# Audio tower kernel: two stages run one after the other, against one unrolled pipeline for both

## The chip, the cores and the metric

The kernel runs on one core of one Trainium2 chip. The metric is the device time of one execution, in microseconds (us); the time before is the median of three runs. Everything else is read from one profiled execution of the same program.

## What is computed

Input `x` has 128 batch rows, 64 features and 750 time steps, all in float32. Three layers follow each other.

```python
# 1. tokens: windows of 8 steps (94 tokens), softmax over the 8 steps, weighted sum
scores = einsum('bwkf,of->bwko', xp, w) + b
pooled = sum(xp * softmax(scores, axis=2), axis=2)          # h: 128 x 94 x 64
# 2. attention, 8 heads of rank 32, on layernorm(h)
q = einsum('btd,hrd->bhtr', x, Q); k = einsum('bud,hrd->bhur', x, K)
attn = softmax(einsum('bhtr,bhur->bhtu', q, k) / sqrt(d))
ctx = einsum('bhtu,bud->bhtd', attn, x)
h = h + einsum('bhtd,hde->bte', ctx, VO)
# 3. a mixture of four experts in four heads, on layernorm(h); its code does not change
h = h + ffn(layernorm(h))
```

## The kernel before

**Units of work.** Four batch rows make a quad, so there are 32 quads (`NQUAD`). Two batch rows make a pair, whose x tile has 128 partitions (2 x 64 features) and 750 columns (375 KB). Eight pairs, or four quads, make a group (`load(G)`, 8 groups). `xs` holds two groups, so the loads of group G wait until TensorE has turned the same slots of group G - 2.

**Order.** Every engine has its own hand-written instruction list, and semaphores tie the lists together. An engine works strictly through its list, so an instruction that waits holds everything behind it. The program has three stages.

- *Tokens*, unrolled, for each quad. TensorE computes the scores of the next group's windows (`tok_score`), transposes the quad's x tiles into three PSUM banks (`turn`), and sums the weighted steps (`pool_x`). VectorE computes the softmax over the 8 steps once per group (`soft_tok`, `norm_tok`) and multiplies the three banks by the weights (`scale_x`). ScalarE copies the pooled tokens to `hj` (`store_h`). Banks 0 to 7 are all used by this stage.
- Then, once, TensorE and ScalarE make small weight products (`g_w` for the attention; `m_s`, `aq`, `wtok`, `wsx` for the experts).
- *Attention*, a software pipeline. Step g works on quads g - 4 to g + 2. The first and last steps are unrolled, and the five middle rounds of four steps are a `Fori` loop. Quads pass through: layernorm on VectorE and GpSimd (`ln_stats`, `ln_power`, `ln_apply`); `turn_x` and `project` on TensorE with copies by ScalarE (`copy_xT`, `copy_k`); three `score` products j = 0, 1, 2 of 8 matmuls each. For j = 0 and 2, VectorE takes the extreme value (`least`) and ScalarE computes eight exponentials straight from PSUM (`exp_s`, eight ACTIVATEs of 94 columns, each with its own bias). For j = 1, VectorE also subtracts, and ScalarE needs one ACTIVATE (`exp_all`). Then row sums and their reciprocals on VectorE (`sums`), the division on GpSimd (`norm_p`), a transposition on VectorE (`turn_p`), the product with the values on TensorE (`mix`), four copies by ScalarE (`copy_cT`), the output product (`give_out`), and the addition to `hj` (`add_out`).
- *Experts*, another such pipeline, which starts after the last `add_out` (`at_added` 32).

The output product reads, for each of the three token blocks j and four head pairs, one 128 x 128 block of `cT` as the stationary operand and moves the 64 columns of `vo_w` through it, in 12 matmuls a quad.
Of the kernel before, what the change touches and what calls it, by code (L numbers as in the profile page):

```python
# [13 lines left out]
KW = 8  # L14
NTOK = -(-NTIME // KW)
TP = 96
# [26 lines left out]
def audio_tower(nc, x, tok_w, tok_b, attn_q, attn_k, attn_vo, hl_w, hl_b, wq, wk, wv, gate_w, gate_b,  # L43
                ln_g, ln_b, fc1_w, fc1_b, fc2_w, fc2_b, fnorm_g, fnorm_b, fgate_w, out):
    with ExitStack() as ctx:
# [51 lines left out]
        tok_pT = sb("tok_pT", [128, TP])  # L97
        x_loaded = [sem(f"x_loaded{i}") for i in range(2 * GP)]
        x_turned = sem("x_turned")
        x_scaled = sem("x_scaled")  # L100
        x_filled = sem("x_filled")
        x_pooled = sem("x_pooled")
        h_pooled = sem("h_pooled")
        tok_scored = sem("tok_scored")
        tok_maxed = sem("tok_maxed")
        tok_biased = sem("tok_biased")
        tok_shifted = sem("tok_shifted")
        tok_exped = sem("tok_exped")
        tok_summed = sem("tok_summed")
        tok_inverted = sem("tok_inverted")  # L110
        tok_normed = sem("tok_normed")
        tok_turned = sem("tok_turned")
        tok_ready = sem("tok_ready")
# [3 lines left out]
        def tok_S(G):  # L117
            return psum[:, G % 2, 0:128]

        def tok_P():  # L120
            return psum[:, 2, 0:TP]

        def x_bank(f):
            return psum[:, 3 + f, :]

        def x_outj(Q):
            return psum[:, 6 + Q % 2, 0:3 * NFEAT]
# [20 lines left out]
        cT = sb("cT", [128, HP, NT, 4, TB])  # L148
        ln_stat = sem("ln_stat")
# [18 lines left out]
        at_cT = sem("at_cT")  # L168
        at_out = sem("at_out")
        at_added = sem("at_added")  # L170
        g_made = sem("g_made")
        g_ready = sem("g_ready")


# [6 lines left out]
        whl2 = kp[0:HD, 0, :, :, :].rearrange("o b h t -> o (b h t)")[:, 0:2 * NH * NFEAT].rearrange("o (n a f) -> o n a f", n=NH, a=2)  # L181
# [58 lines left out]
        w_made = sem("w_made")  # L240
        w_read = sem("w_read")
# [78 lines left out]
        def _(sp):  # L320

            def load(G):
                for p in range(GP):
                    slot = GP * (G % 2) + p
                    if positive(GQ * (G - 2) + p // 2 + 1):
                        sp.wait_ge(x_turned, GQ * (G - 2) + p // 2 + 1)
# [9 lines left out]

            def slow(dst, src):
# [3 lines left out]
            for n in range(NH):  # L341
                load(2 + n)
# [4 lines left out]
            load(2 + NH)  # L347
# [12 lines left out]
            load(3 + NH)  # L360
# [43 lines left out]
        def _(pool):  # L404
# [57 lines left out]
            def attention(q):  # L462
                for v in range(4):
                    g = 4 * q + v
                    if exists(g - 1, NQUAD):
                        pool.wait_ge(at_summed2, 2 * g)
                        norm_p(2)
                        pool.wait_ge(at_summed1, 2 * g)
                        norm_p(1)
# [3 lines left out]
                    if exists(g, NQUAD):  # L473
                        pool.wait_ge(at_summed0, 2 * g + 2)
                        norm_p(0)
                    if exists(g + 2, NQUAD):
                        pool.wait_ge(ln_rstd, 2 * g + 6)
                        if exists(g + 1, NQUAD):
                            pool.wait_ge(at_turned, g + 2)
# [4 lines left out]
            pool.wait_ge(h_pooled, NQUAD)  # L484
            for q in range(-1, 2):
                attention(q)
            with pool.Fori(2, 7) as q:
                attention(q)
            for q in range(7, 9):
                attention(q)  # L490

# [107 lines left out]
        def _(pe):  # L599

            def turn(G, Q, f):

                n = GQ * G + Q
                if positive(n):
                    pe.wait_ge(x_scaled, 3 * (n - 1) + f + 1)
                for i in range(4):
                    pair, c = (f, i) if f < 2 else (i // 2, 4 + i % 2)
                    mm = pe.transpose(x_bank(f)[:, 128 * i:128 * i + 128],  # L608
                                      xs[:, GP * (G % 2) + 2 * Q + pair, 128 * c:128 * c + 128], ident)
                if f == 2:  # L610
                    mm.then_inc(x_turned, 1)
                else:
                    mm.then_inc(x_filled, 1)
# [1125 lines left out]
```

## Time and profile before

| | us |
|---|---|
| median of three runs (1123.84 to 1126.86) | 1125.67 |
| time of the profiled execution | 1129.79 |
| its span, first to last instruction | 1128.0 |
| tokens, up to the last `store_h` | 0 to 144.0 |
| weight products and attention, up to the last `add_out` | 144.0 to 518.3 |
| experts | 518.3 to 1128.0 |
| TensorE, VectorE, ScalarE, GpSimd busy | 985.3, 931.5, 674.2, 676.0 |

PE is TensorE's matmul row, DVE is VectorE, ACT is ScalarE, POOL is GpSimd, SP issues the loads. The profile records each float32 matmul of this kernel as two instructions, and each transposition as one. Matmuls are pipelined, so their rows overlap; the distance from one row's start to the next row's start says how long a group holds the engine.

### The profile page before, as it was taken

How to read it: one execution, taken by the hardware profiler on the slowest of the kernel's cores; microseconds unless marked ns; L12 is line 12 of the kernel's file. 1: busy time of each engine (PE TensorE's matmuls, PEld its weight loads, DVE VectorE, ACT ScalarE, POOL GpSimd, SP SyncE). 2: the span in 40 equal slices, each digit the busy share in tenths (PEclk: the TensorE clock that was granted, in tenths of full speed). 3: DMA queues.
4: the chain of work that ended last, by engine and by line, in shares of the span. 5: the costliest groups of instructions: out<-in, count | busy, mean ns of one | idle time of the engine just before them, and what ended most of it. 6: DMA issues, size and time to landing. Idle time of an engine off the chain costs nothing.

```text
span 1128.0 us, 40703 instructions
## 1 busy us (share of the span) xinstructions
PE 985.3 (87%) x16376; PEld 681.6 (60%) x16376; DVE 931.5 (83%) x2061; ACT 674.2 (60%) x1719; POOL 676.0 (60%) x991
## 2 busy tenths in 40 slices
PE   5889878898898988986899999999999999999952
PEld 4667644454454544544677677777777776777741
DVE  3565539999999999982799999999999999999852
ACT  0111137777777777761666767767767667667621
POOL 2000036666656666541048788788888887788786
PEclk9999869999999999996899999999999999999975
DMA  7664300000000000000000001000000000010000
GB/s 256 192 207 125 113 1 2 2 2 2 1 0 0 0 0 0 2 1 6 15 10 15 16 15 23 18 16 20 14 15 19 11 20 18 12 22 19 20 8 14
DMA packets 41576, 35.31 MB, mean 31 GB/s; under 512 B 28160, under 2 KB 31232, under 8 KB 41472
## 3 DMA queue, kind: packets, MB, share of 16 engines
q1 hardware_dynamic: 41376, 33.83, 10.9%
q8 instruction: 77, 1.26, 0.5%
q14 instruction: 27, 0.22, 0.1%
q0 software_dynamic: 96, 0.00, 0.0%
HBM read 24.95 MB, written 3.08 MB: 25 GB/s over the span
## 4 chain that ended last, share of the span: by engine, by line
PE 48%; DVE 25%; POOL 12%; issue 8%; ACT 4%; DMA 1%; DVEq 1%; POOLq 0%; SPq 0%; ACTq 0%
PE psum L733 8%; DVE mx L1569 5%; PE psum L716 4%; PE psum L608 4%; PE psum L623 3%; DVE yc L1611 3%; PE psum L870 3%; PE psum L708 3%; PE psum L881 3%; PE psum L885 3%; PE psum L726 3%; POOL pu L459 3%; DVE xn L1561 2%; PE psum L855 2%; PE psum L889 2%
## 5 line engine op out<-in xcount | busy, mean ns | idle before, releaser
L459 POOL TENSOR_TENSOR pu<-pu,pr 128x752 f32<-128x752 f32 x96 | 138.7, 1444 | 127.7 <-DVE pr L1490 127.7
L524 POOL TENSOR_TENSOR st<-st,neg_half 128x12 f32<-128x12 f32 x64 | 145.8, 2278 | 5.0
L1189 ACT ACTIVATE pu<-psum,mx 128x94 f32<-128x94 f32 x512 | 124.6, 358 | 15.7 <-DVE mx L1481 14.5
L1272 ACT ACTIVATE pT<-psum 96x512 f32<-96x512 f32 (+1 forms) x224 | 126.4, 594 | 6.2 <-PE psum L870 3.3
L1569 DVE TENSOR_REDUCE mx<-psum 128x16 f32<-128x1536 f32 (+2 forms) x96 | 116.6, 1215 | 15.7 <-PE psum L855 11.5
L870 PE MATMUL psum<-ident_w,pu 128*96 128x128 f32 (+1 forms) x896 | 119.9, 275 | 1.9 <-ACT pT L1272 1.5
L1572 DVE TENSOR_TENSOR pu<-psum,mx 128x1536 f32<-128x1536 f32 (+2 forms) x96 | 117.6, 1225 | 3.3
L1266 ACT ACTIVATE pu<-pu 128x1536 f32<-128x1536 f32 (+2 forms) x96 | 101.8, 1060 | 10.0 <-DVE pu L1572 8.2
L733 PEld LDWEIGHTS psum<-vo_w,cT 128*128 128x128 f32 x768 | 90.7, 196 | 24.4 <-issue 13.0
L870 PEld LDWEIGHTS psum<-ident_w,pu 128*96 128x96 f32 (+1 forms) x896 | 100.8, 135 | 6.9 <-ACT pT L1272 4.3
L1422 DVE TENSOR_TENSOR xt<-psum,tok_pT 128x512 f32<-128x512 f32 x96 | 61.4, 684 | 50.5 <-PE psum L608 50.2
L1276 ACT ACTIVATE oc<-psum 128x336 f32<-128x336 f32 x96 | 43.2, 450 | 98.8 <-PE psum L896 96.1
L733 PE MATMUL psum<-vo_w,cT 128*128 128x64 f32 x768 | 95.2, 282 | 4.4 <-ACT cT L1198 4.3
L896 PE MATMUL psum<-gx,ct 128*128 128x84 f32 x768 | 97.9, 277 | 0.0
L896 PEld LDWEIGHTS psum<-gx,ct 128*128 128x128 f32 x768 | 90.6, 192 | 6.3 <-ACT kp L1253 6.0
L1481 DVE TENSOR_REDUCE mx<-psum 128x8 f32<-128x752 f32 x96 | 87.1, 908 | 6.7 <-PE psum L716 6.7
L445 POOL TENSOR_TENSOR ln_ve<-ln_mv,eps_c 128x3 f32<-128x3 f32 x32 | 6.2, 192 | 138.9 <-DVE ln_mv L1475 138.9
L1198 ACT ACTIVATE cT<-psum 128x384 f32<-128x384 f32 x128 | 59.6, 495 | 49.9 <-PE psum L726 49.9
L1494 DVE STREAM_TRANSPOSE pT<-pu 128x768 f32<-128x768 f32 x96 | 88.6, 948 | 0.7 <-POOL pu L459 0.7
L1488 DVE TENSOR_REDUCE pl<-pu 128x8 f32<-128x752 f32 x96 | 88.3, 920 | 1.0 <-ACT pu L1189 0.5
L716 PE MATMUL psum<-kp,xT 64*32 64x376 f32 x1536 | 83.7, 496 | 1.0 <-ACT kp L1182 1.0
L819 PE MATMUL psum<-x3T,aq 64*128 64x384 f32 x256 | 81.7, 527 | 3.1
(178 smaller groups left out, 2324.8 us busy)
## 6 DMA issues: line engine op xcount, KB each, us to landing
xs<-in_x SPq DMA_DIRECT2D x64, 375.0 KB, 4.4
vb<-va SPq DMA_DIRECT2D x32, 128.0 KB, 2.3
out_h<-ho SPq DMA_DIRECT2D x128, 16.0 KB, 1.4
out_h<-ho SPq DMA_DIRECT2D x128, 7.5 KB, 1.4
vc<-va SPq DMA_DIRECT2D x96, 16.0 KB, 1.8
gx<-in_L_ffn_gate_w SPq DMA_DIRECT2D x16, 0.2 KB
fc<-in_L_ffn_fc_w SPq DMA_DIRECT2D x12, 1.0 KB
fc<-in_L_ffn_fc_b SPq DMA_DIRECT2D x12, 0.1 KB
```

The costliest lines, as they stand in the source:

```text
L459: pool.tensor_tensor(p, p, bcast(pr[:, j, :, :].rearrange("p a b -> p (a b)"), 2, NTOK), ALU.mult).then_inc(at_normed, 1)
L524: pool.tensor_tensor(st[:, k, 3, :], st[:, k, 2, :], neg_half[:, 0:NJ * NH], ALU.pow).then_inc(rstd, 1)
L716: mm = pe.matmul(psum[TB * b:TB * b + TB, (low, high)[par], 0:HP * NTOK], xT[rows, p, b, TB * j:TB * j + TB], kp[rows, p, b, :, 0:NTOK], s ...
L733: mm = pe.matmul(psum[:, bank, NFEAT * j:NFEAT * j + NFEAT], cT[:, hp, j, :, :].rearrange("p b t -> p (b t)"), vo_w[:, hp, :], start=(hp = ...
L870: mm = pe.transpose(psum[0:rows, bank, 128 * e:128 * e + 128], src, ident)
L896: mm = pe.matmul(psum[:, bank, GC * e:GC * e + GC], ct3[:, i, 2 * (e % 2) + e // 2 if i == 1 else e, :], gx[:, e, :], start=True, stop=True)
L1189: ins = act.activation(pu[:, j, par, hp, 0:NTOK], psum[:, (low, high)[par], NTOK * hp:NTOK * hp + NTOK], ACT.Exp, bias=mx[:, j, par, hp:hp ...
L1266: act.activation(p, p, ACT.Exp).then_inc(s_exped, 1)
L1272: act.activation(pT3[j][:, f - (0, 4, 6)[i], :, :, :].rearrange("p e b t -> p (e b t)"), psum[0:rows, bank, :], ACT.Copy).then_inc(p_copie ...
L1494: dve.transpose(pT[:, j, :, :, :, :].rearrange("p a h u t -> p (a h u t)"), pu[:, j, :, :, :].rearrange("p a h u -> p (a h u)")).then_inc( ...
L1569: dve.tensor_reduce(mx3[:, i, :, :], S3(j), AX.X, ALU.max).then_inc(shifted, 1)
L1572: dve.tensor_tensor(p, S3(j), bcast(mx3[:, i, :, :], 3, QB * (j + 1)), ALU.subtract).then_inc(shifted, 1)
```

## The change

Tokens and attention become one pipeline on every engine, written out for all its 48 steps (`quad(q)` for q from -2 to 9, g = 4q + v), with no loop. In step g TensorE computes `tok_score(g + 7)`, `turn(g + 3, 0)`, `turn(g + 2, 1)`, `turn(g + 2, 2)` and `pool_x(g + 1)` among the attention work of quads g down to g - 4. The order inside a step, the distances between steps and the PSUM banks are all new. Tokens' scores have bank 0 to themselves, `tok_pT` is doubled, and the weight products are made inside steps (`make_g` at g = -4, `make_w` and `make_w2` at g = 12 and 13).

Two computations change their form. `exp_s` now also writes the row sums `pl` through `accum_out`, so `sums` of j = 0 and 2 keeps only its reciprocal. The output product is turned round: `give_outT` holds `vo_w` still and moves 192 columns of `cT`, `copy_oT` brings the transposed result to SBUF, and the new `give_out` transposes it back with six 64 x 64 products.

The loads change their order: `load(1)` comes behind the attention's weights, `load(2)` and `load(3)` among the experts' weights, and groups 4 to 7 behind all of them.

```diff
-            load(1)
             sp.dma_start(q_w[:, :, :], attn_q.rearrange("h r d -> r h d")).then_inc(attn_loaded, 16)
...
+            load(1)
+
...
-                load(2 + n)
+                if n == 0:
+                    load(2)
...
-            load(2 + NH)
+            load(3)
...
+            for G in range(4, NGROUP):
+                load(G)
...
+            def give_outT(bank):
+
+                for hp in range(HP):
+                    for half in range(2):
+                        mm = pe.matmul(psum[64 * half:64 * half + 64, bank, 0:NT * 64].rearrange("p (j c) -> p j c", j=NT), vo_w[:, hp, :],
+                                       cT[:, hp, :, 2 * half:2 * half + 2, :].rearrange("p j b t -> p j (b t)"),
+                                       start=(hp == 0), stop=(hp == HP - 1))
+                mm.then_inc(at_outT, 1)
+
             def give_out(bank):
                 for j in range(NT):
-                    for hp in range(HP):
-                        mm = pe.matmul(psum[:, bank, NFEAT * j:NFEAT * j + NFEAT], cT[:, hp, j, :, :].rearrange("p b t -> p (b t)"), vo_w[:, hp, :],
-                                       start=(hp == 0), stop=(hp == HP - 1))
+                    for half in range(2):
+                        rows = slice(64 * half, 64 * half + 64)
+                        mm = pe.matmul(psum[rows, bank, NFEAT * j:NFEAT * j + NFEAT], oT[rows, j, :, :].rearrange("p b t -> p (b t)"),
+                                       ident[rows, 64 * half:64 * half + 64], start=True, stop=True)
                 mm.then_inc(at_out, 1)
...
                         ins = act.activation(pu[:, j, par, hp, 0:NTOK], psum[:, (low, high)[par], NTOK * hp:NTOK * hp + NTOK], ACT.Exp,
-                                             bias=mx[:, j, par, hp:hp + 1], scale=-1.0)
+                                             bias=mx[:, j, par, hp:hp + 1], scale=-1.0, accum_out=pl[:, j, par, hp:hp + 1])
...
+            def copy_oT(bank):
+                act.activation(oT[:, :, :, :].rearrange("p j b t -> p (j b t)"), psum[:, bank, 0:NT * 64], ACT.Copy).then_inc(at_oT, 1)
...
-                dve.tensor_reduce(pl[:, j, :, :], pu[:, j, :, :, 0:NTOK], AX.X, ALU.add).then_inc(done, 1)
-                dve.wait_ge(done, 2 * g + 1)
+                if j in (1,):
+                    dve.tensor_reduce(pl[:, j, :, :], pu[:, j, :, :, 0:NTOK], AX.X, ALU.add).then_inc(done, 1)
+                    dve.wait_ge(done, 2 * g + 1)
                 dve.reciprocal(pr[:, j, :, :], pl[:, j, :, :]).then_inc(done, 1)
```

The order of a full step is set by the new `quad(q)` of each engine. Three waits in it tie the engines together where the prediction speaks of them. On TensorE, `mix` of quad g - 3 waits for both `exp_s` of quad g - 2 (they free banks 1 and 2) and for `least(1)` of quad g - 2 (it frees banks 4 and 5); `score(0)` of quad g - 1 needs the four `kp` copies of that quad, two of which follow the `project` that follows `mix`. On ScalarE, `exp_s(0)` waits for `least(0)` (`at_maxed0`).

```diff
+                    if exists(g - 3, NQUAD):
+                        pe.wait_ge(at_pturned, 3 * g - 6)
+                        if exists(g - 2, NQUAD):
+                            pe.wait_ge(at_exped, 3 * g - 4)
...
+                        if exists(g - 2, NQUAD):
+                            pe.wait_ge(at_maxed1, 2 * g - 2)
...
+                        mix((v + 1) % 4, (1, 2, 4, 5))
...
+                    if exists(g - 1, NQUAD):
+                        pe.wait_ge(at_q, 4 * g)
...
+                        score((v + 1) % 2, 0, 6, 7)
```

TensorE before, first a quad of the tokens stage (L608 transposes x, L623 scores tokens, L635 pools), in the unrolled part of the program.

```order
8 L608 MATMUL psum<-ident_w,xs 128x128 x12
9 L623 MATMUL psum<-xs,tw 32x128 x12
10 L635 MATMUL psum<-xt,pick 32x192 x8
11 L608 MATMUL psum<-ident_w,xs 128x128 x12
12 L635 MATMUL psum<-xt,pick 32x192 x8
```

TensorE before, a full step of the attention (L702 `turn_x`, L716 `score`, L708 `project`, L733 `give_out`, L726 `mix`).

```order
142 L702 MATMUL psum<-ident_w,xn 128x128 x3
143 L716 MATMUL psum<-kp,xT 32x376 x8
144 L708 MATMUL psum<-xT,g_w 128x384 x2
145 L716 MATMUL psum<-kp,xT 32x376 x8
146 L733 MATMUL psum<-vo_w,cT 128x64 x12
147 L716 MATMUL psum<-kp,xT 32x376 x8
148 L726 MATMUL psum<-pT,xn 64x384 x24
149 L708 MATMUL psum<-xT,g_w 128x384 x2
```

TensorE of the change, one full step (L706 `give_outT`, L680 `project`, L624 `tok_score`, L698 `mix`, L715 the new `give_out`, L612 `turn`, L632 `pool_x`, L688 `score`, L674 `turn_x`).

```order
71 L706 MATMUL psum<-cT,vo_w 64x192 x8
72 L680 MATMUL psum<-xT,g_w 128x384 x2
73 L624 MATMUL psum<-xs,tw 32x128 x12
74 L698 MATMUL psum<-pT,xn 64x384 x24
75 L680 MATMUL psum<-xT,g_w 128x384 x2
76 L715 MATMUL psum<-ident_w,oT 64x64 x6
77 L612 MATMUL psum<-ident_w,xs 128x128 x4
78 L632 MATMUL psum<-xt,pick 32x192 x8
79 L688 MATMUL psum<-kp,xT 32x376 x8
80 L674 MATMUL psum<-ident_w,xn 128x128 x3
81 L612 MATMUL psum<-ident_w,xs 128x128 x8
82 L688 MATMUL psum<-kp,xT 32x376 x16
```

The token work of one quad now stands between the attention products of other quads, and the first `score` of a quad stands behind `mix`, `project`, `give_out`, `turn` and `pool_x`.

ScalarE before, one full step of the attention (L1189 the exponentials, L1182 `kp` copies, L1198 `cT` copies, L1195 `exp_all`, L1178 `xT`).

```order
52 L1189 ACTIVATE pu<-psum,mx 128x94 x8
53 L1182 ACTIVATE kp<-psum 128x4x96
54 L1189 ACTIVATE pu<-psum,mx 128x94 x8
55 L1198 ACTIVATE cT<-psum 128x3x4x32 x2
56 L1182 ACTIVATE kp<-psum 128x4x96 x2
57 L1195 ACTIVATE pu<-pu 128x8x94
58 L1198 ACTIVATE cT<-psum 128x3x4x32
59 L1178 ACTIVATE xT<-psum 128x3x4x32
60 L1198 ACTIVATE cT<-psum 128x3x4x32
61 L1182 ACTIVATE kp<-psum 128x4x96
```

ScalarE of the change, one full step (L1286 the exponentials with their sums, L1279 `kp`, L1292 `exp_all`, L1300 `copy_oT`, L1295 `cT`, L1258 `store_h`, L1275 `xT`).

```order
81 L1275 ACTIVATE xT<-psum 128x3x4x32
82 L1286 ACTIVATE pu,pl<-psum,mx 128x94 x16
83 L1279 ACTIVATE kp<-psum 128x4x96
84 L1292 ACTIVATE pu<-pu 128x8x94
85 L1300 ACTIVATE oT<-psum 128x192
86 L1279 ACTIVATE kp<-psum 128x4x96
87 L1295 ACTIVATE cT<-psum 128x3x4x32 x2
88 L1279 ACTIVATE kp<-psum 128x4x96 x2
89 L1295 ACTIVATE cT<-psum 128x3x4x32 x2
90 L1258 ACTIVATE hj<-psum 128x192
```

The sixteen exponentials of a quad now stand in one piece, each with a second output, and two copies of 192 columns are new in the step.

## Rows read from the trace of the kernel before

**Rows 1.** Busy time by stage: tokens, attention, experts

```profile
11.30:144.00 132.70, 115.04 (x1684) 92.59 (x1685) 74.00 (x151) 14.23 (x48) 0.00 (x0) 0.92 0.55 170
144.00:518.30 374.30, 325.41 (x4265) 179.37 (x4261) 326.22 (x672) 266.58 (x837) 216.80 (x256) 0.95 0.00 1
518.30:1128.00 609.70, 544.83 (x10432) 409.68 (x10432) 527.64 (x1216) 392.07 (x833) 452.70 (x704) 0.95 0.08 16
```

**Rows 2.** Timeline of PE, one attention step: start, duration, group, idle before

```profile
344.29 0.86 PE L716 MATMUL psum<-kp,xT 64*32 64x376 f32 x16
345.08 2.89 PE L733 MATMUL psum<-vo_w,cT 128*128 128x64 f32 x24
347.90 0.86 PE L716 MATMUL psum<-kp,xT 64*32 64x376 f32 x16
348.72 2.19 PE L726 MATMUL psum<-pT,xn 32*64 32x384 f32 x48
350.85 0.92 PE L708 MATMUL psum<-xT,g_w 64*128 64x384 f32 x4
352.94 0.54 PE L702 MATMUL psum<-ident_w,xn 128*128 128x128 f32 x3 [1.18 <-POOL xn L454]
...
354.21 0.92 PE L708 MATMUL psum<-xT,g_w 64*128 64x384 f32 x4
355.06 0.86 PE L716 MATMUL psum<-kp,xT 64*32 64x376 f32 x16
```

**Rows 3.** The same step: span, busy PE, PEld, DVE, ACT, POOL, clock, DMA

```profile
344.29:355.06 10.77, 9.60 (x134) 5.20 (x132) 10.21 (x23) 8.29 (x26) 6.77 (x8) 1.00 0.00 0
```

**Rows 4.** Timeline of PE, one quad of the tokens stage

```profile
75.00 1.53 PE L608 MATMUL psum<-ident_w,xs 128*128 128x128 f32 x12
76.46 0.97 PE L623 MATMUL psum<-xs,tw 128*32 128x128 f32 x21
...
77.34 0.84 PE L635 MATMUL psum<-xt,pick 128*32 128x192 f32 x15
78.11 1.53 PE L608 MATMUL psum<-ident_w,xs 128*128 128x128 f32 x12
```

**Rows 5.** Groups of instructions, VectorE and ScalarE, tokens stage: busy, mean ns, idle

```profile
L1422 DVE TENSOR_TENSOR xt<-psum,tok_pT 128x512 f32<-128x512 f32 x96 | 61.4, 684 | 50.5 <-PE psum L608 50.2
...
L1402 DVE TENSOR_TENSOR tok_e<-tok_e,tok_r 96x128 f32<-96x128 f32 x8 | 2.3, 286 | 0.3
...
L1148 ACT ACTIVATE hj<-psum 128x192 f32<-128x192 f32 x32 | 10.6, 330 | 93.5 <-PE psum L635 93.5
```

**Rows 6.** Groups of instructions, VectorE, 200 to 480 us

```profile
L1488 DVE TENSOR_REDUCE pl<-pu 128x8 f32<-128x752 f32 x78 | 71.7, 919 | 0.0
L1481 DVE TENSOR_REDUCE mx<-psum 128x8 f32<-128x752 f32 x78 | 70.9, 909 | 0.0
```

**Rows 7.** Timeline of ScalarE, one attention step

```profile
345.21 1.95 ACT L1189 ACTIVATE pu<-psum,mx 128x94 f32<-128x94 f32 x8 [0.32 <-DVE mx L1481]
347.00 0.54 ACT L1182 ACTIVATE kp<-psum 128x384 f32<-128x384 f32 x1
```

**Rows 8.** ScalarE's group of exponentials over the run: duration min, median, max

```profile
L1189 ACT ACTIVATE pu<-psum,mx x512: 330/357/471, 163.0 to 499.4; 128x94 f32<-128x94 f32 x171
```

**Rows 9.** Timeline of ScalarE in the experts stage, its smallest instruction

```profile
710.69 0.20 ACT L1296 ACTIVATE fe<-fl 128x12 f32<-128x12 f32 x1
710.79 0.97 ACT L1253 ACTIVATE kp<-psum 128x384 f32<-128x384 f32 x2
```

**Rows 10.** Timeline of PE at the start of the tokens stage

```profile
11.38 6.10 PE L623 MATMUL psum<-xs,tw 128*32 128x128 f32 x96 [11.38 <-DMA tokb<-in_L_tok_b]
19.86 0.42 PE L643 MATMUL psum<-ident_w,tok_e 96*128 96x96 f32 x1 [2.38 <-DVE tok_e L1402]
```

**Rows 11.** Timeline of PE at the end of the attention

```profile
492.59 1.50 PE L716 MATMUL psum<-kp,xT 64*32 64x376 f32 x32 [0.97 <-ACT kp L1182]
```

**Rows 12.** Timeline of DVE, the last addition to `hj`

```profile
517.91 0.36 DVE L1499 TENSOR_TENSOR hj<-psum,hj 128x192 f32<-128x192 f32 x1 [10.28 <-PE psum L733]
```

More of the change, by code:

```diff
@@ L482, in attention @@
                         ln_apply(g + 2, (v + 2) % 4)
[L484 to L490, printed above, removed]
+                    if exists(g, NQUAD):
+                        pool.wait_ge(at_summed1, 2 * g + 2)
+                        norm_p(1)
+            for q in range(-2, 10):
+                quad(q)
             def power3(g):
@@ L665, in _ @@
-            pool_x(NQUAD - 1)
-            pe.wait_ge(x_scaled, 3 * NQUAD)
-            pe.wait_ge(tok_ready, NGROUP)
-            pe.wait_ge(attn_loaded, 16 * 4)
-            for half in range(2):
-                for i in range(2):
-                    for par in range(2):
-                        hd = 2 * (2 * i + half) + par
-                        mm = pe.matmul(psum[64 * half:64 * half + 64, 0, 64 * (2 * i + par):64 * (2 * i + par) + 64],
-                                       k_w[:, hd, :], q_w[:, hd, :], start=True, stop=True)
@@ L793, in attention @@
-                    if exists(g + 1, NQUAD):
-                        score((v + 1) % 2, 0, 4, 5)
-                    if exists(g + 2, NQUAD):
-                        pe.wait_ge(at_xT, g + 3)
-                        project(v % 2, 0, 0, 2)
-                    if exists(g + 1, NQUAD):
-                        score((v + 1) % 2, 2, 6, 7)
-            pe.wait_ge(h_pooled, NQUAD)
-            for q in range(-1, 2):
-                attention(q)
-            with pe.Fori(2, 7) as q:
-                attention(q)
@@ L806, in _ @@
-            for q in range(7, 9):
-                attention(q)
+                            pe.wait_ge(at_xT, g)
+                        score((v + 1) % 2, 2, 1, 2)
+                    if g + 4 == 0:
+                        pe.wait_ge(tok_ready, ((g + 4) // 4) + 1)
+                        make_g()
+            for q in range(-2, 10):
+                quad(q)
             pe.wait_ge(causal_set, 10)
@@ new lines, in quad @@
+                    if exists(g - 2, NQUAD):
+                        act.wait_ge(at_maxed2, g - 1)
+                        exp_s(2, 1, 2)
+                    if exists(g - 1, NQUAD):
+                        act.wait_ge(at_pb, g)
+                        copy_k((v + 1) % 2, 2, 6)
+                    if exists(g - 2, NQUAD):
+                        act.wait_ge(at_maxed1, 2 * g - 2)
+                        exp_all(1)
+                    if exists(g - 4, NQUAD):
+                        act.wait_ge(at_outT, g - 3)
+                        copy_oT(3)
@@ L1244, in front_xT @@
+                    if exists(g - 3, NQUAD):
+                        copy_cT(1, 2)
+                    if g + 3 == 0:
+                        if exists(g + 3, NQUAD):
+                            act.wait_ge(g_made, 1)
+                        copy_g()
+                    if exists(g - 3, NQUAD):
+                        copy_cT(2, 4)
+            for q in range(-2, 10):
+                quad(q)
             def front_xT(bank):
```

654 lines of the change are left out of this document (371 added, 283 removed).

## The prediction

> **What bounds the kernel now.** I first cut the span into its three stages [rows 1]. Tokens take 132.7 us after TensorE's first matmul at 11.38 us, attention 374.3 us, experts 609.7 us. The change leaves the experts' code alone, so their 609.7 us stay; what can move is the 518.3 us before them. The reader should see that the two stages have opposite habits. In the tokens stage TensorE is busy 115 of 132.7 us, VectorE 74, ScalarE 14 and GpSimd 0. In the attention all four work, but the stage starts empty and ends empty.
>
> A full attention step [rows 3] lasts 10.77 us. VectorE is busy 10.21 of it, TensorE 9.60, ScalarE 8.29, GpSimd 6.77. TensorE's timeline [rows 2] gives each group by start-to-start distances: a `score` 0.80, `give_out` 2.82, `mix` 2.13, a `project` 0.85, `turn_x` 0.47, and one gap of 1.18 us in which it waits for the layernorm. So VectorE and TensorE bound the step together. With 32 quads at 10.77 us the stage would take 345 us; the other 30 us are the weight products, filling and draining.
>
> In the tokens stage a quad needs 3.11 us of TensorE [rows 4]: transposes 1.46, `tok_score` 0.88, `pool_x` 0.77. VectorE's `scale_x` waits 50.2 us for TensorE there and works 61.4 us [rows 5]. The loads move 170 GB/s at a DMA share of 0.55 [rows 1], so they are not the bound even now; spread over the whole pipeline they need well under half of that rate.
>
> **TensorE after.** Per step: 9.60 without the old output product (2.82) is 6.78. Add the tokens' 3.11. The new output product isn't in the trace; `give_outT` has 8 matmuls that move 192 columns. The nearest row is `pool_x`, also 8 matmuls of 192 columns, which takes 0.77 us with four column quarters side by side, that is two rounds. `give_outT` has two column halves, four rounds: 1.5 us. Below, 1.3; above, if the halves did not run beside each other, eight rounds, 3.1. The new `give_out` has 6 products of 64 x 64 in pairs; the old one took 2.82 / 12 = 0.235 us a matmul, so 0.5, between 0.35 (three pairs at half that) and 1.4. Sum 6.78 + 3.11 + 1.5 + 0.5 = 11.9 us a step.
>
> **VectorE after.** 10.21, minus two row sums of 0.92 [rows 6], plus three `scale_x` of 0.684 [rows 5], plus a group's six small softmax instructions of about 0.29 each [rows 5] over four quads, 0.4: 10.8 us. Below TensorE.
>
> **ScalarE after.** 8.29, plus `store_h` 0.33 [rows 5], `copy_oT` of the same width 0.33, the tokens' exponential and copy 0.15: 9.1, plus 16 times the price a of a summed exponential. The trace has no `accum_out`. Without it eight exponentials take 1.79 us start to start [rows 7], 0.224 each, though each lasts 0.357 [rows 8]: neighbours overlap by 0.133. Sums leave the engine's accumulator by an extra write. The smallest ScalarE instruction [rows 9] has 12 columns, lasts 0.20, and the next starts 0.10 after it. So a lies between 0 (no instruction of its own) and 0.33 (0.20 for the write, and the lost overlap 0.133). I take 0.15, between the 0.10 that the row costs its neighbour and the 0.20 that it lasts. ScalarE's load is then 11.5 us a step.
>
> The Trainium skill, "ScalarE: Activation LUTs", section "What ACT_TABLE_LOAD costs", puts an ACTIVATE with immediate operands at 186 ns plus 0.83 ns a column, with 93 ns of overlap between neighbours. If the sum's write is such an instruction of one column, a would be an estimated 0.09 us by that page and the step about 1 us shorter than my sum has it; its 186 ns agree with the 0.20 row [rows 9].
>
> **The loop that sets the step.** Loads alone give 11.9. But the new order ties TensorE and ScalarE into a ring. `exp_s(0)`, `exp_s(2)` of quad g - 2 must end before `mix` of quad g - 3 (it takes their banks). Behind `mix` stand `project`, `give_out`, `turn`, `pool_x`, and only then `score(0)` of quad g - 1, then `least(0)`, then the next `exp_s(0)`. Length: exponentials 16 x 0.224 + 16 x 0.15 = 5.98; `mix` 2.13; `project` 0.85; `give_out` 0.5; `turn` of four transposes 1.46 / 3 = 0.49; `pool_x` 0.77; `score` 0.80; `least` 0.91 [rows 6]; three hand-offs between engines at 0.1 (the exponentials wait 0.32 from the start of their idle time for `least` [rows 7], the most that I would allow in sum). That is 12.7. Every fourth step VectorE has the group's softmax ahead of `least(0)` and ScalarE an exponential, about 1.1 us, 0.3 a step. The step is 13.0 us: TensorE waits 1.1 of it in front of `mix`. Queued behind `mix` is all of the above, the `cT` copies and VectorE's `least(0)`; nothing else fills that time, since TensorE's list is fixed.
>
> **The sum.** The start is as before up to the first group's transposed weights, 19.86 [rows 10]; the weight product for the attention follows at once. Then steps g = -3 to 0 are short chains (transposes, `scale_x`, `pool_x`, layernorm), 1.5 + 3 + 4 + 7 us, to about 36. Step 1 adds `project`, the `kp` copies and two scores, 8 us; step 2 the exponentials, 11; step 3 `mix`, 12: full steps begin near 67. Steps 4 to 24 are full, 21 x 13.0 = 273. Steps 25 to 31 lose `tok_score`, the group softmax and later the turns, but keep the ring: 7 x 12.7 = 89. Step 32 has no new quad, 10.5. Then the last quad drains. Before, from the end of the last `score` pair at 494.1 [rows 11] to the last addition's end at 518.27 [rows 12] took 24.2 us; the new output product is shorter and the granted clock as low, 22. Sum 67 + 273 + 89 + 10.5 + 22 = 461.5, against 518.3: 56.8 us less. The weight products of 9 us hide in steps 12 and 13 but for a little, which the sum takes as nothing (their cover is the wait ahead of `mix`; without it, 3 us more). From the profiled execution's 1129.8 that leaves 1073.0. The median of the runs shown is 4.1 us below that execution, so I predict 1069 us.
>
> **Moved DMAs.** The attention's four weight loads now stand before the second group, whose first pair is needed right behind the attention product at about 22 us; a few us of delay there are inside the range. Slots come free three steps, over 30 us, before they are needed again, so later loads are hidden, and the small experts' loads behind `load(3)` are needed only in step 12.
>
> **Rivals.**
> - *The ring is short and TensorE bounds* (the summed exponentials cost 0.10 or less): 11.9 to 12.1 a step. 28 steps x 1.0 less: 1069 - 28 = 1041. For it: the 0.10 of [rows 9]. Against it: a write that reads what the instruction before it has just summed may not overlap like two strangers. Chance 0.2.
> - *The ring is longer*, with a at 0.20 (0.8 us a step), or `give_outT`'s halves one after the other (TensorE 13.5), or VectorE late with `least(0)`, since its own load leaves 2 us: 13.6 to 14.8 a step, 1086 to 1119. Chance 0.2.
> - *Slower than before*: the sum's write waits for its exponential to end and the next waits for the write, a = 0.33. The ring is 13.0 + 16 x 0.18 = 15.9 us, 28 x 2.9 = 81 us more: 1150. It decides from a = 0.28, where the step is 15.0 and the gain of 57 us is spent. Against it: the neighbours of [rows 7] overlap although each has its own bias. Chance 0.07.
> - *The pipeline gains nothing from the merge* since TensorE's instructions, now unrolled, arrive late while x is loaded: the tokens stage was unrolled too, with the loads at a share of 0.55, and TensorE was busy 115 of 132.7 us [rows 1]. Chance 0.02, about 1125.
>
> **How the numbers follow.** The forecast, a step of 12.4 to 13.6 us (1052 to 1086), has a chance of 0.48; its own range is that. 0.03 is left for a step that is still shorter or a faster start. The range takes in the TensorE-bound case and most of the longer ring: 1037 to 1105. What a measurement of this kernel can tell from no change is about 0.3%, 3.4 us. Faster by over 0.3%: 0.91; within it 0.02; slower 0.07.
>
> **What would show it.** The experts' start near 462 us (518.3 before) and their length unchanged; a step of 13.0 us between two `mix` groups; TensorE idle about 1 us ahead of `mix`, released by ScalarE's exponentials; eight summed exponentials in 3.0 us; `give_outT` 1.5 us. Wrong would be: a step under 12.2 with TensorE never waiting, a wait for VectorE ahead of `score` or the exponentials, or `give_outT` near 3.

## The result and the profile after

| | before | after |
|---|---|---|
| median of four executions | 1124.97 us | 1058.18 us |
| their spread | 1123.84 to 1126.86 | 1055.77 to 1060.38 |
| profiled execution, its own time | 1129.8 us | 1060.38 us |
| its span | 1128.0 us | 1058.6 us |
| start of the experts stage | 518.3 us | 446.1 us |

The changed kernel is faster, ratio 0.940 (95% interval 0.938 to 0.943). It came out 11 us below the forecast of 1069 us, inside its range.

First, from the page of after, the two groups of a summed exponential, then the group of `mix` (columns: busy, mean ns, idle before and its releaser).

```profile
L1286 ACT ACTIVATE pu<-psum,mx 128x94 f32<-128x94 f32 x512 | 164.6, 374 | 4.5 <-DVE mx L1583 2.3
...
L1286 ACT ACTIVATION_READ_ACCUMULATOR pu<-psum,mx 128x1 f32 x512 | 123.8, 242 | 0.0
...
L698 PE MATMUL psum<-pT,xn 32*64 32x384 f32 x1536 | 72.6, 502 | 22.0 <-ACT pu L1286 22.0
```

A summed exponential is two instructions: the ACTIVATE and a read of the accumulator, 512 of each. And all that TensorE waits ahead of `mix` in the whole run, 22.0 us, it waits for these exponentials.

Next, a full step of after between two `mix` groups, the stretch in one row (the columns are those of [rows 3]), then the chain of waits through the same step.

```profile
250.05:262.17 12.12, 11.78 (x188) 6.70 (x188) 10.52 (x24) 10.19 (x45) 6.73 (x8) 1.00 0.20 65
```

```profile
250.05 2.19 PE psum L698 x48
252.25 0.84 PE psum L680 x4
253.09 0.49 PE psum L715 x12
253.59 0.59 PE psum L612 x4
254.18 0.79 PE psum L632 x16
254.96 0.88 PE psum L688 x16
...
255.86 0.95 DVE mx L1583
...
256.84 5.24 ACT pu L1286 x32
262.08 0.09 issue
262.17 2.19 PE psum L698 x48
```

Reading down: `mix`, `project`, `give_out`, `turn`, `pool_x`, `score(0)`, `least(0)`, sixteen summed exponentials, the next `mix`. This is the ring of the prediction, member for member, and it lasts 12.12 us. TensorE is busy 11.78 of it, so it is only 0.34 short of being the bound itself. Two `mix` groups are 12.12 apart in all but a few of the full steps; every fourth is 12.35, and one of these is 18.62 (the weight products). The 0.23 us more of the fourth step is one member more in the ring, TensorE's `tok_turn` between `pool_x` and `score(0)`:

```profile
230.50 0.23 PE psum L637
```

The price of a sum is read from ScalarE's timeline, start to start.

```profile
256.84 0.34 ACT L1286 ACTIVATE pu<-psum,mx 128x94 f32<-128x94 f32 x1
257.07 0.19 ACT L1286 ACTIVATION_READ_ACCUMULATOR pu<-psum,mx 128x1 f32 x1
257.17 0.33 ACT L1286 ACTIVATE pu<-psum,mx 128x94 f32<-128x94 f32 x1
...
261.87 0.57 ACT L1279 ACTIVATE kp<-psum 128x384 f32<-128x384 f32 x1
```

Sixteen take 261.87 - 256.84 = 5.03 us, 0.314 each, against 0.224 without the read [rows 7]. The read lasts 0.19 to 0.29 us, but the exponential behind it starts 0.10 after the read's start: a = 0.09. The estimate that the prediction worked out from the Trainium skill, "ScalarE: Activation LUTs", section "What ACT_TABLE_LOAD costs" (186 ns less 93 ns of overlap), was 0.09 too. The trace agrees on that distance; the read itself lasts longer than 186 ns, 241 ns in the median of all 512.

`give_outT`, on TensorE's timeline of that step:

```profile
258.46 1.52 PE L706 MATMUL psum<-cT,vo_w 128*64 128x192 f32 x16
259.91 0.92 PE L680 MATMUL psum<-xT,g_w 64*128 64x384 f32 x4
```

`give_outT` takes 1.45 from its start to the next group's, the new `give_out` 0.49 (in the chain above), together 1.94 where the old product took 2.82 [rows 2].

Last, VectorE's last addition to `hj`, which answers to [rows 12]: its end at 446.09 is where the experts start.

```profile
445.73 0.36 DVE L1602 TENSOR_TENSOR hj<-psum,hj 128x192 f32<-128x192 f32 x1 [3.48 <-PE psum L715]
```

### The profile page after: what moved, and what is told of

It is laid out like the page before. It is cut to its first block, busy times and chain, and to the rows that moved or that the text cites. A ratio compares the mean times of both kernels' runs of the same rounds, so it can differ in the third digit from the quotient of the medians.

```text
span 1058.6 us, 41021 instructions
## 1 busy us (share of the span) xinstructions
PE 945.7 (89%) x16504; PEld 641.0 (61%) x16504; DVE 881.5 (83%) x1997; ACT 723.9 (68%) x2263; POOL 675.7 (64%) x991
## 3 DMA queue, kind: packets, MB, share of 16 engines
q8 instruction: 95, 1.56, 0.6%
## 4 chain that ended last, share of the span: by engine, by line
PE 42%; DVE 24%; ACT 16%; POOL 8%; issue 7%; DMA 1%; DVEq 1%; POOLq 0%
ACT pu L1286 15%; PE psum L698 7%; DVE mx L1685 5%; DVE yc L1727 3%; PE psum L985 3%; PE psum L996 3%; PE psum L1000 3%; PE psum L688 3%; DVE mx L1583 3%; PE psum L680 3%; PE psum L1004 3%; DVE xn L1677 2%; PE psum L970 2%; PE psum L632 2%; PE psum L612 2%
## 5 line engine op out<-in xcount | busy, mean ns | idle before, releaser
L472 POOL TENSOR_TENSOR pu<-pu,pr 128x752 f32<-128x752 f32 x96 | 138.7, 1445 | 137.8 <-DVE pr L1593 137.8
L1286 ACT ACTIVATE pu<-psum,mx 128x94 f32<-128x94 f32 x512 | 164.6, 374 | 4.5 <-DVE mx L1583 2.3
L1286 ACT ACTIVATION_READ_ACCUMULATOR pu<-psum,mx 128x1 f32 x512 | 123.8, 242 | 0.0
L1597 DVE STREAM_TRANSPOSE pT<-pu 128x768 f32<-128x768 f32 x96 | 92.9, 970 | 7.6 <-PE psum L698 5.0
L698 PE MATMUL psum<-pT,xn 32*64 32x384 f32 x1536 | 72.6, 502 | 22.0 <-ACT pu L1286 22.0
L1696 DVE SCALAR_TENSOR_TENSOR ct<-sxT,psum 128x512 f32<-128x512 f32 x96 | 65.2, 680 | 24.1 <-PE psum L1004 17.3
L688 PE MATMUL psum<-kp,xT 64*32 64x376 f32 x1536 | 76.2, 487 | 2.7 <-ACT xT L1275 1.6
L1295 ACT ACTIVATE cT<-psum 128x384 f32<-128x384 f32 x128 | 55.9, 497 | 26.4 <-PE psum L698 26.4
L970 PE MATMUL psum<-kp,sxT 32*32 32x256 f32 (+2 forms) x3072 | 69.3, 390 | 0.0
```

The source lines that it names most:

```text
L472: pool.tensor_tensor(p, p, bcast(pr[:, j, :, :].rearrange("p a b -> p (a b)"), 2, NTOK), ALU.mult).then_inc(at_normed, 1)
L688: mm = pe.matmul(psum[TB * b:TB * b + TB, (low, high)[par], 0:HP * NTOK], xT[rows, p, b, TB * j:TB * j + TB], kp[rows, p, b, :, 0:NTOK], s ...
L698: mm = pe.matmul(psum[64 * par:64 * par + 64, banks[b], 0:HP * TP], xn[rows, r, ub, 0, :], pT[rows, :, par, :, ub, :], start=(ub == 0), st ...
L1286: ins = act.activation(pu[:, j, par, hp, 0:NTOK], psum[:, (low, high)[par], NTOK * hp:NTOK * hp + NTOK], ACT.Exp, bias=mx[:, j, par, hp:hp ...
```

## The experiments

Nine kernels ran, and the changed kernel once more (changed_again). Times differ a little from chip to chip, so each is given as a ratio to the kernel before on the same chip. The steps are distances between two `mix` groups in one profiled execution of each.

| kernel | full step | group's step | ratio | 95% interval |
|---|---|---|---|---|
| changed kernel | 12.12 | 12.35 | 0.9404 | 0.9379 to 0.9429 |
| no_sums | 11.79 | 12.02 | 0.9246 | 0.9208 to 0.9283 |
| sums_on_vector | 12.76 | 14.8 to 16.3 | 0.9716 | 0.9666 to 0.9766 |
| old_product | 12.58 | 14.04 | 0.9581 | 0.9544 to 0.9619 |
| merge_alone | 12.58 | 14.57 | 0.9658 | 0.9641 to 0.9675 |
| sums_alone (old stages) | 10.77 | | 1.0017 | 1.0001 to 1.0034 |
| late_pool | 11.97 | 12.68 | 0.9366 | 0.9328 to 0.9403 |
| late_w | 12.12 | 12.35 | 0.9340 | 0.9322 to 0.9358 |
| late_w_late_pool | 11.97 | 12.69 | 0.9346 | 0.9325 to 0.9367 |
| late_split | 12.12 | 12.35 | 0.9363 | 0.9348 to 0.9379 |
| changed_again | 12.13 | 12.37 | 0.9388 | 0.9375 to 0.9401 |

### Is it the ring through ScalarE? (no_sums)

The row sums of j = 0 and 2 are left out, and the softmax's denominators are 1 there.

```diff
-                                             bias=mx[:, j, par, hp:hp + 1], scale=-1.0, accum_out=pl[:, j, par, hp:hp + 1])
+                                             bias=mx[:, j, par, hp:hp + 1], scale=-1.0)
...
+            dve.memset(pl[:, :, :, :], 1.0).then_inc(zeroed4, 1)
```

> Edit: the changed kernel with the exponentials' accum_out taken away and nothing in its place (the row sums of j = 0 and 2 are a constant 1, so the division of these rows is left out of the result). It prices the summed exponentials. Theory A (the ring from the exponentials over mix, project, give_out, turn, pool_x, score and least back to the exponentials sets the step of 12.12 us): the ring loses 16 x 0.09 = 1.44 us and would be 10.7, so TensorE's own load of 11.8 sets the step; 28 to 31 steps x 0.33 less, 9 to 10 us: 1048 us. Theory B (TensorE's load already sets the step, and its wait of 0.34 ahead of mix is only a hand-off): no change, 1058 us. In the trace A wants TensorE's wait ahead of mix gone and the step at 11.8.

Measured: 1042.82 us, ratio 0.9246. The stretch between two `mix` groups:

```profile
242.57:254.36 11.79, 11.78 (x188) 6.70 (x188) 10.51 (x23) 9.02 (x29) 6.75 (x8) 1.00 0.21 67
```

The step is TensorE's load to 0.01 us, and nothing waits ahead of `mix`. So the ring binds with the sums and TensorE without them, and the two are 0.33 us apart. The reads put 16 x 0.09 = 1.44 us into the ring but cost 0.33 a step, because the rest lay under TensorE's load. The time is 5 us under theory A's 1048. Of the 18.8 us between the two spans, 12.2 lie between the first and the last `mix` (the last two distances gain 1.2 and 1.6, not 0.33), 3.2 ahead of the first, and 3.2 in the experts. These last 3.2 are not the sums' work: the experts' code is the same, and their time varies by that much from execution to execution (below).

### The same sums on VectorE (sums_on_vector)

```diff
-                if j in (1,):
-                    dve.tensor_reduce(pl[:, j, :, :], pu[:, j, :, :, 0:NTOK], AX.X, ALU.add).then_inc(done, 1)
-                    dve.wait_ge(done, 2 * g + 1)
+                dve.tensor_reduce(pl[:, j, :, :], pu[:, j, :, :, 0:NTOK], AX.X, ALU.add).then_inc(done, 1)
+                dve.wait_ge(done, 2 * g + 1)
```

The exponentials lose their `accum_out` as in no_sums, and the counts in GpSimd's waits follow.

> Edit: the changed kernel with the row sums of j = 0 and 2 back on VectorE (two reductions of 0.93 us a step), exponentials without accum_out. Theory A (each engine's load bounds when the ring is short): VectorE's 10.52 us becomes 12.38, so the step is 12.4 to 12.7 and the time 1066 to 1075 us. Theory B (only the ring counts, and it gets 1.44 us shorter while VectorE's added work hides): TensorE bounds at 11.8, 1048 us.

Measured: 1097.72 us, ratio 0.9716, slower than forecast. The row of a step, and the VectorE part of its chain:

```profile
270.99:283.75 12.76, 11.78 (x188) 6.69 (x188) 12.13 (x25) 9.02 (x29) 6.74 (x8) 1.00 0.18 61
```

```profile
276.80 0.94 DVE mx L1583
277.74 1.20 DVE xt L1532 x2
...
280.77 0.83 DVE pl L1590
...
282.66 0.95 DVE pu L1586
```

VectorE now has 12.13 us of work in 12.76, and the ring runs through its list from `least(0)` to the next `mix`; no exponential is in it. A plain step loses only 0.64 us. Between the first and the last `mix` the kernel takes 44.0 us more than the changed kernel. The plain steps are 10 of them. The last nine steps are 13: six `mix` groups there took 3.5 to 3.9 us instead of 2.19, at the lower clock. The largest part, 21, is in the group's steps, which last 14.8 to 16.3 where the changed kernel takes 12.35 (and 22.8 for 18.62 with the weight products).

Two things make the group's steps long. VectorE has nothing spare for the group's softmax, and one instruction of it, `tok_mb` on a tile of 96 x 16, lasts 1.39 us here where it lasts 0.23 in the changed kernel. GpSimd's `norm_p` (L472) runs beside it and ends 0.02 us before it. First sums_on_vector, VectorE's row and GpSimd's, then the changed kernel:

```profile
245.21 1.39 DVE L1509 TENSOR_SCALAR tok_mb<-tok_m,tokb 96x16 f32<-96x16 f32 x1
245.14 1.44 POOL L472 TENSOR_TENSOR pu<-pu,pr 128x752 f32<-128x752 f32 x1
```

```profile
226.13 0.23 DVE L1509 TENSOR_SCALAR tok_mb<-tok_m,tokb 96x16 f32<-96x16 f32 x1
```

The two group's steps of 14.8 us ran at the full clock, those of 16.3 did not: in the second row below TensorE took 3.72 us from the first `score` to the end of `turn` (mean granted clock 0.55), in the first 2.15.

```profile
243.38:258.22 14.84, 12.26 (x188) 6.75 (x189) 14.52 (x31) 9.23 (x31) 6.78 (x8) 1.00 0.17 54
349.64:365.92 16.28, 12.79 (x165) 7.04 (x165) 14.82 (x31) 9.19 (x31) 6.78 (x8) 0.90 0.00 2
```

### The old output product in the new pipeline (old_product)

```diff
-                        give_outT(3)
+                        give_out(3)
...
-                    for half in range(2):
-                        rows = slice(64 * half, 64 * half + 64)
-                        mm = pe.matmul(psum[rows, bank, NFEAT * j:NFEAT * j + NFEAT], oT[rows, j, :, :].rearrange("p b t -> p (b t)"),
-                                       ident[rows, 64 * half:64 * half + 64], start=True, stop=True)
+                    for hp in range(HP):
+                        mm = pe.matmul(psum[:, bank, NFEAT * j:NFEAT * j + NFEAT], cT[:, hp, j, :, :].rearrange("p b t -> p (b t)"), vo_w[:, hp, :],
+                                       start=(hp == 0), stop=(hp == HP - 1))
...
-                        copy_oT(3)
```

The old call of `give_out(7)` between `project` and `turn` goes, and VectorE's `add_out` moves to the end of its step, since the sum is there later.

> Edit: the changed kernel with the old output product (12 matmuls, cT stationary) at give_outT's place in the step, into bank 3; copy_oT and the six turning products are gone, and add_out stands at the end of VectorE's step. TensorE's load is 11.78 - 1.45 - 0.49 + 2.82 = 12.66 us, while the ring loses 0.49. Theory A (two bounds, the longer one sets the step): step 12.7, 0.55 us x 28 to 31 more, 1073 to 1076 us. Theory B (only the ring counts): step 11.6 to 11.8, 1044 to 1049 us.

Measured: 1080.89 us, ratio 0.9581. The row of a step:

```profile
264.07:276.65 12.58, 12.58 (x187) 7.80 (x184) 10.35 (x22) 9.98 (x44) 6.80 (x9) 1.00 0.19 62
```

TensorE is busy through the whole step, and later, where `tok_score` has ended, the step falls to 11.64. This is plain TensorE bound: the new product takes 0.80 us off TensorE's load (12.58 to 11.78), which puts it under the ring, and the step gains 0.46 of that. The time is 5 to 8 us above theory A's, and the group's steps, which A left out, are the larger part of that: each is 1.46 us longer than a plain one. TensorE stands at `tok_turn` there for the end of VectorE's softmax, in which `tok_mb` lasts 1.49 us beside `norm_p`, 1.26 more than in the changed kernel.

### The merge alone, and the sums alone

merge_alone is the pipeline with the edits of sums_on_vector and old_product together, so with neither companion computation. sums_alone is the kernel before, in its two stages, with this edit only (and the counts in GpSimd's waits that follow from it):

```diff
-                                             bias=mx[:, j, par, hp:hp + 1], scale=-1.0)
+                                             bias=mx[:, j, par, hp:hp + 1], scale=-1.0, accum_out=pl[:, j, par, hp:hp + 1])
...
+                if j in (1,):
+                    dve.tensor_reduce(pl[:, j, :, :], pu[:, j, :, :, 0:NTOK], AX.X, ALU.add).then_inc(done, 1)
```

> The one pipeline with neither companion edit: all row sums on VectorE and the old output product at its old place. Theory A: VectorE's load is the one of sums_on_vector (12.1 busy in a step of 12.77), TensorE's that of old_product (12.58), and the two form one ring without ScalarE's accumulator: 12.9 to 13.6 us a step, with group steps of 15 to 16; 1090 to 1110 us, ratio 0.97 to 0.985. Theory B: the merge is where nearly all of the gain is, the rest is small: as old_product, ratio 0.955 to 0.965.

> The kernel before with one edit: the row sums of j = 0 and 2 come with ScalarE's exponentials, all else as it was (two stages). Theory A: VectorE (10.21 busy of 10.77) was the nearer bound of the attention step and loses 1.84; ScalarE gains 16 x 0.09 = 1.4 to 9.7, TensorE stays at 9.6: the step falls to 9.7 to 10.1, 32 x 0.8 = 26 us less, ratio 0.973 to 0.98. Theory B: TensorE's wait of 1.18 us for the layernorm stays because the ring there runs through the exponentials as well, which are 1.4 longer: step 10.6 to 10.8, ratio 0.995 to 1.0.

Measured: merge_alone 1088.26 us, ratio 0.9658; sums_alone 1128.39 us, ratio 1.0017, no gain. A step of merge_alone, then one of sums_alone:

```profile
267.15:279.73 12.58, 12.58 (x187) 7.80 (x184) 12.01 (x26) 8.70 (x28) 6.74 (x8) 1.00 0.19 62
```

```profile
337.29:348.06 10.77, 9.59 (x140) 5.16 (x132) 8.65 (x19) 9.63 (x44) 6.80 (x9) 1.00 0.00 0
```

merge_alone's ratio lies at the border of theory B's range, and A had its plain step wrong: it is TensorE's 12.58, not VectorE's. In sums_alone VectorE has lost 1.56 us of work and the step has not moved (10.77). The chain of waits through its step tells why, and it holds no VectorE and no ScalarE work at all:

```profile
339.82 0.51 POOL xc L450
...
340.41 0.98 POOL xn L454 x2
341.39 0.12 issue
341.51 0.54 PE psum L702 x3
...
344.49 2.82 PE psum L733 x24
347.31 0.79 PE psum L716 x16
348.10 2.22 PE psum L726 x48
```

The old step was TensorE's 9.59 and 1.18 of waiting for GpSimd's `xc` and `xn`, which start behind the end of `mix`. Both theories for sums_alone had a wrong picture: A took VectorE for the nearer bound, B put the exponentials into the ring. It also shows what the merge did: its plain step of 12.58 is all TensorE, so the 1.18 went to token work.

Four kernels with the pipeline make a square. With the old product the sums on ScalarE bring 0.8% (0.9658 to 0.9581). With the new product they bring 3.1% (0.9716 to 0.9404). With the sums on ScalarE the new product brings 1.8%. With the sums on VectorE it brings nothing: 0.9716 against 0.9658, with plain steps of 12.76 against 12.58. These ratios hold the group's steps and the stretches at the lower clock too. The plain steps alone say the same: 12.58 with either place of the sums under the old product, 12.76 and 12.12 under the new one. The new product puts `give_out` between `mix` and `score(0)`, into the ring, so TensorE's shorter list pays only if the ring has room for it.

### The order inside the step (late_pool)

`pool_x` and `tok_turn` go from ahead of the first `score` to behind it.

```diff
+                    if exists(g - 1, NQUAD):
+                        pe.wait_ge(at_q, 4 * g)
...
+                        score((v + 1) % 2, 0, 6, 7)
                     if exists(g + 1, NQUAD):
                         pe.wait_ge(x_scaled2, g + 2)
...
-                        score((v + 1) % 2, 0, 6, 7)
```

> Edit: the changed kernel with pool_x and tok_turn moved behind the first score of the step on TensorE; no work is added or taken away. Theory A (the ring sets the step): pool_x's 0.79 us leave the ring, VectorE's transposition and scale_x then hold least back, so the ring is 11.3 to 11.7 and TensorE's load of 11.8 sets the step: 9 to 10 us less, 1048 us. Theory B (TensorE's load sets it already): no change, 1058 us.

Measured: 1056.25 us, ratio 0.9366: the median is under the changed kernel's 0.9404, but the intervals overlap, so the step tells more. The chain of its step:

```profile
253.12 0.83 PE psum L688 x16
253.96 0.79 PE psum L632 x16
254.74 0.49 PE psum L674 x3
...
255.26 0.49 ACT xT L1275
255.75 5.13 ACT pu L1286 x32
```

`pool_x` was 0.79 us of the ring, but only 0.15 came off (11.97), and the group's step grew to 12.68. `score(0)` is early now, and still `pool_x` and `turn_x` are in the ring, since ScalarE's list has the copy of `xT` ahead of the exponentials. An instruction comes out of a ring only where it leaves every engine's list between two members.

### The weight products (late_w, late_split)

late_w moves `make_w` to step 33 and `make_w2` behind the last step; VectorE's `split_w` goes to step 30. late_split is late_w with `split_w` in step 32.

```diff
-                    if g + 3 == 16:
-                        if exists(g - 13, NQUAD):
-                            pe.wait_ge(w_read, 1)
-                        make_w2()
...
+                    if g == 33:
+                        pe.wait_ge(tok_ready, NGROUP)
+                        pe.wait_ge(w_split, 1)
+                        make_w()
...
+            pe.wait_ge(w_read, 1)
+            make_w2()
```

> The expert weight products (the two tiny ones and the sixteen small ones), which stand inside step 12 to 13 of the changed kernel, are moved behind the last score, where TensorE waits for ScalarE in the drain. Theory A: the one step of 18.6 us there is 6.5 us longer than its neighbours because nothing in the ring covers the products, and in the drain part of them fills waits of 3.5 to 3.7 us: the step falls to 12.1 to 12.4, the drain grows by 0 to 2 us, total 4 to 6 us under the changed kernel, ratio to the kernel before 0.935 to 0.937. Theory B: the products' time is only moved (the drain grows by 5 to 6 us, since the last quad's chain waits behind them): ratio as the changed kernel's, 0.939 to 0.942.

> Both moves at once: weight products behind the last score, and tokens' pooling and turning behind the attention's first score. If the two savings are of different places they add: about 3 us (late_pool) and 5 us (late_w) under the changed kernel, ratio to the kernel before 0.931 to 0.934. If the later score makes ScalarE's list late in the drain, only the larger remains: 0.935 to 0.937.

late_w_late_pool has the edits of late_w and of late_pool.

> As late_w, with VectorE's preparation of the expert weights (split_w: two copies and two subtractions, 2.47 us) at step 32 and not at step 30. Theory A: in late_w this work stood ahead of VectorE's turn_p(2), scale_x and least(0), so TensorE waited 1.30 us for scale_x, that step took 14.1 us, and the granted clock fell to 0.56 in the next mix (3.80 us for 2.13): step 32 has no scale_x left, so 2 to 3.5 us come back, ratio to the kernel before 0.931 to 0.933. Theory B: the clock falls anyway in this part and the delay only moves to step 32: as late_w, 0.934.

> The changed kernel once more, beside late_split and in the same rounds of the kernel before, as the mark for the small differences of the last runs: ratio 0.938 to 0.942 as measured first. If it is at 0.942 or above on this chip, late_w's and late_pool's gains are larger than read so far, if under 0.937 they are not told from nothing.

Measured: late_w 0.9340, late_w_late_pool 0.9346, late_split 0.9363 beside changed_again's 0.9388. The long step is gone in all three. Between the first and the last `mix`, late_w takes 373.3 us, late_split 371.5 and late_w_late_pool 371.4, against 377.4 in the changed kernel. What late_w gave back is in its chain, ahead of the exponentials of one of the last steps:

```profile
381.35 0.07 DVE whl L1530
381.42 0.66 DVE whl L1531
382.08 1.33 DVE whl L1530
383.41 0.32 DVE whl L1531
```

`split_w` itself, 2.5 us with its last instruction, stands between the addition to `hj` and `least(0)`. That step took 14.08 us, and the `mix` behind it ran at the lower clock (3.80 us instead of 2.19, below). More than half of the 2.5 us is the copy of 16 x 4 elements that takes 1.33: `norm_p` runs beside it, and it ends 0.02 us behind `norm_p`. In late_split the chain through step 32 has the same copy of 1.33 us on it, at 403.73 us.

So theory A of late_split was wrong in its place: `split_w` is not off the path there, where the step takes 13.40 us instead of 11.36. The delay of 2.0 us only moved, as B has it, and what came back, 1.8 us between the first and the last `mix`, answers to the `mix` that kept the full clock (1.6 us). These are differences of single traces: by its median late_split has a ratio of 0.9363, above both theories' figures and not told from late_w's 0.9340 (the intervals overlap). Against changed_again on the same chip it is 1052.42 to 1056.83 us, 0.4% less. The sixteen small products behind the last step were not free either, since the experts' first product waits behind them. It starts 3.17 us after the last addition in the changed kernel, 4.02 in late_split and 5.56 in late_w, where the second half of the products ran at the lower clock; VectorE then waits 2.81 us instead of the usual 1.2. late_w's experts take 614.3 us and late_split's 610.9, but how much of that is the products is not shown, since this time varies by 3.7 us without them (below). The savings of late_w and late_pool add between the first and the last `mix` (4.1 and 1.9 us, together 6.0), not in the total, where the experts of that execution took 615.2 us. The versions between 0.934 and 0.937 are a little faster than the changed kernel; which of them is best these runs can't tell.

## Why the prediction was nearly right, step by step

It forecast 1073.0 us for the profiled execution and 1069 for the median; they are 1060.4 and 1058.2.

- **"The loop that sets the step": right.** The chain shows it member for member. Only `tok_turn`, 0.23 us in every fourth step, is missing from it. The step was 12.12 us and not 13.0, which lies below the forecast's own range of 12.4 to 13.6. The step of the prediction that failed is the price a of a summed exponential, taken as 0.15 "between the 0.10 that the row costs its neighbour and the 0.20 that it lasts". It measured 0.09: -0.96 us a step. What counts is the lower of these, the distance to the neighbour. The estimate from the Trainium skill's page was the better one, and the prediction set it aside.
- **The other members of the ring** were 0.35 us too short in sum: `turn` 0.59 for 0.49, `score` 0.88 for 0.80, the last exponential's whole length, less one hand-off. Only the last ends of a group count in a ring, and they are longer than the start-to-start distances that I added up.
- **The group's softmax** was put at 0.3 us a step. It cost nothing: VectorE had 1.6 us of room in the step (10.52 busy of 12.12). The 0.23 us of every fourth step, 0.06 a step, are `tok_turn`'s.
- **TensorE's load** was forecast at 11.9 and is 11.78; `give_outT` 1.5 and 1.45, `give_out` 0.5 and 0.49. VectorE 10.8 and 10.52. ScalarE 11.5 and 10.19, 0.96 of the 1.31 from a.
- **"The weight products of 9 us hide ... the sum takes as nothing": wrong.** That step is 18.62 us, 6.5 more than its neighbours. On TensorE's timeline the sixteen small products run from 179.89 to 183.56 and their forerunner (L654) takes 0.88, 4.55 us in all. The cover was the wait ahead of `mix`, which is 0.34 and not the 1.1 of the forecast. And the next stretch, `score` and `give_outT`, ran at a granted clock of 0.56 and took 3.83 us where it takes 2.16 in the step shown above. The forecast's other value, 3 us without cover, was too low as well:

```profile
179.89 0.43 PE L661 MATMUL psum<-m_s,whl 16*128 16x64 f32 x2
...
183.56 1.50 PE L688 MATMUL psum<-kp,xT 64*32 64x376 f32 x16
184.99 2.47 PE L706 MATMUL psum<-cT,vo_w 128*64 128x192 f32 x16
```

```profile
183.56:187.39 3.83, 3.83 (x34) 1.84 (x33) 2.19 (x5) 3.23 (x19) 0.46 (x1) 0.56 0.00 0
```

- **"VectorE and TensorE bound the step together" (of the kernel before): wrong.** sums_alone shows it. It was TensorE and GpSimd's `xn`; VectorE's 10.21 of 10.77 was load beside the path. This sentence didn't enter the sum, so it cost the prediction nothing, but it would have misled whoever had tried the sums alone first.
- **The sum by stretches.** The first 68.7 us (67 forecast), 21 full steps 262.2 (273; 6.5 of them the weight products), seven steps 83.4 (89), the rest 31.8 (32.5): 446.1 against 461.5. The experts took 612.5 and not 609.7. From 1003 to 1012 us TensorE ran at a granted clock of 0.50 there, in changed_again, whose experts took 610.2, at 1.00. In the eight other executions that have the same experts' code and nothing new ahead of it they took 609.2 (late_pool) to 612.9 us (sums_alone), so this is spread. It did hide a fifth of the error.
- **The rivals.** "TensorE bounds", 11.9 to 12.1 a step, is nearer to what came than the forecast's ring: the ring is 0.34 above TensorE's load. Its condition, a of 0.10 or less, was met; its 1041 us wasn't, since the ring then is 12.1 and not under 11.9, and since the weight products stood open. no_sums is that rival in pure form: 1042.8 us. That the time fell into the forecast's own range owes something to errors of opposite sign: -0.9 us a step, +6.5 for the weight products, +2.8 for the experts.

Open: why TensorE's clock fell in four of the six group's steps of sums_on_vector and not in the two of 14.8 us, whose waits are the same 0.85 and 0.59 us. A late `pool_x` together with the copy of `xT` behind the exponentials, which late_pool's chain points to, wasn't tried.

## What to carry to other kernels

When in-order engines hand work round, write the ring down with each engine's list between two members, and compare its length with each load: here they were 0.34 us apart, so each half of the change pays in full only with the other (the sums 0.8% alone and 3.1% with the new product, the new product nothing alone and 1.8% with the sums). An engine at 95% of a step need not bound it: take work away from it alone and look, as in sums_alone, or read the chain of waits rather than the busy shares. Work taken as hidden needs a named cover of its size on each engine; where the cover is a wait that the same change shortens, price the work in full. A merged order also sets which instructions of two engines run side by side: look for one whose duration has grown, as `tok_mb`'s from 0.23 to 1.39 us.

## What the runs showed of the hardware

A sum through `accum_out` is an instruction of its own, which lasts 0.19 to 0.29 us and costs 0.09 between neighbours of 94 columns, though it reads what the one before it has just summed.

VectorE's `tok_mb`, 96 x 16, lasts 0.23 us wherever `norm_p` does not run beside it. In all 18 places where it does (six each in sums_on_vector, old_product and merge_alone) it lasts 1.13 to 1.50 and ends 0.02 to 0.04 us after `norm_p`, whichever of the two started first. That it waits for GpSimd's instruction is read from these ends; no run moved that instruction alone.

TensorE's granted clock fell from full speed to 0.56, so for most of that stretch the lower of its two levels (1.2 GHz of 2.4), right after sixteen products of 16 and 64 columns in which TensorE was busy without a gap by the profile (the two rows above). In late_w it fell to the same 0.56 in a `mix` that took 3.80 us instead of 2.19, behind waits of 0.58 and 1.60; in late_split and in the changed kernel the first `mix` of the drain took 3.9 to 4.2, behind waits of 2.8 and 3.7. Here are the row of the changed kernel and late_w's:

```profile
430.16 4.15 PE L698 MATMUL psum<-pT,xn 32*64 32x384 f32 x48 [3.69 <-ACT pu L1286]
```

```profile
391.49 3.80 PE L698 MATMUL psum<-pT,xn 32*64 32x384 f32 x48 [1.60 <-ACT pu L1282]
```

Yet late_split ran a `mix` at 2.19 behind a wait of the same 1.60:

```profile
412.54 2.19 PE L698 MATMUL psum<-pT,xn 32*64 32x384 f32 x48 [1.60 <-ACT pu L1282]
```

So the length of the last wait alone doesn't tell whether the clock falls. The group's steps of sums_on_vector say the same.
